# Attention scores from two fp32r parts of q and k, two heads in the two row halves of the array

## The reference, cut to what matters

```python
q = q * cos + _rotate_half(q) * sin
k = k * cos + _rotate_half(k) * sin
scores = jnp.einsum('bhqd,bhkd->bhqk', q, k) / math.sqrt(hd)
scores = jnp.where(causal[None, None], -jnp.inf, scores)
attn = jax.nn.softmax(scores, axis=-1)
attn_out = jnp.einsum('bhqk,bhkd->bhqd', attn, v)
```

## Time and profile before

| what | value |
|---|---|
| median of 3 runs | 2708.45 us (2705.41 to 2710.56) |
| span of the profiled execution, first to last instruction | 2663.3 us |
| that execution's own time | not listed apart from its span; the median stands 45.1 us above the span |
| busy: PE, DVE, ACT, GpSimd | 90%, 78%, 55%, 14% |
| projection, about | 0 to 363 us |
| routing and first max jobs, about | 363 to 437 us |
| attention loop | 437 to 2146 us |
| expert and dense networks | 2146 to 2663 us |

### The profile page before, as it was taken

One profiled execution on the slowest core, in us unless ns is written; L12 is line 12 of the kernel. 1 busy time (PEld: TensorE's weight loads), 2 busy tenths in 40 slices (PEclk: granted clock), 3 DMA queues, 4 the chain that ended last, 5 costly groups with the idle time before them and its releaser, 6 DMA issues. The chain is left out here.

```text
span 2663.3 us, 49751 instructions
## 1 busy us (share of the span) xinstructions
PE 2394.4 (90%) x14968; PEld 1211.4 (45%) x14968; DVE 2072.5 (78%) x3856; ACT 1463.1 (55%) x1762; POOL 377.9 (14%) x319
## 2 busy tenths in 40 slices
PE   0999947999999999998899999999999868886998
PEld 0889942333333333232333333333322247776888
DVE  7888889999999988562799999988864257776776
ACT  2444513566666666777566666666677733332443
POOL 2111149500000000000000000000000023333344
PEclk9999977999999999999999999999999979998999
DMA  4122247300000021000410000003100144443232
GB/s 123 64 95 91 90 114 186 104 9 9 9 9 1 9 50 43 13 10 17 92 30 9 9 9 9 1 9 70 28 9 9 22 115 126 126 126 97 64 95 71
DMA packets 158629, 144.79 MB, mean 54 GB/s; under 512 B 36448, under 2 KB 142176, under 8 KB 158304
## 3 DMA queue, kind: packets, MB, share of 16 engines
q1 hardware_dynamic: 155360, 133.94, 18.9%
q0 software_dynamic: 3072, 8.39, 0.9%
HBM read 95.61 MB, written 46.66 MB: 53 GB/s over the span
## 5 line engine op out<-in xcount | busy, mean ns | idle before, releaser
L883 DVE TENSOR_REDUCE attn_MX<-psB 128x1 f32<-128x512 f32 (+3 forms) x2352 | 1357.2, 638 | 352.5 <-PE psB L756 223.2
L869 ACT ACTIVATE attn_PB<-psB 128x1024 f32<-128x1024 f32 (+3 forms) x1152 | 1035.8, 950 | 563.9 <-PE psB L788 509.7
L756 PE MATMUL psB<-attn_KS,attn_QS 96*128 96x512 bf16 (+3 forms) x2352 | 764.5, 370 | 51.5 <-DVE attn_MX L883 44.9
L788 PE MATMUL psB<-attn_QS,attn_KS 104*128 104x512 bf16 (+3 forms) x2304 | 652.6, 363 | 24.5 <-ACT attn_QS L846 16.0
L803 PE MATMUL psB<-attn_PB,attn_V 128*32 128x512 f32 (+3 forms) x4608 | 579.8, 570 | 0.0
L756 PEld LDWEIGHTS psB<-attn_KS,attn_QS 96*128 96x128 bf16 x2352 | 200.6, 97 | 639.8 <-DVE attn_MX L883 522.2
L788 PEld LDWEIGHTS psB<-attn_QS,attn_KS 104*128 104x128 bf16 x2304 | 210.2, 98 | 336.1 <-ACT attn_PB L869 128.9
L1043 POOL TENSOR_TENSOR W1L<-W,W1H 128x512 fp32r<-128x512 f32 x36 | 53.8, 1524 | 1664.3 <-ACT W1H L1120 1664.3
L803 PEld LDWEIGHTS psB<-attn_PB,attn_V 128*32 128x32 f32 x4608 | 96.3, 108 | 175.9 <-issue 166.8
L759 PE MATMUL psB<-attn_mask_qk,attn_idb 128*128 128x128 bf16 x544 | 119.2, 227 | 0.0
L42 PE MATMUL ps_experts<-W2H,HH_experts 128*128 128x256 f32 x256 | 83.9, 328 | 35.1 <-DVE Y_experts L1233 20.3
(11 more groups left out here) (213 smaller groups left out, 3216.5 us busy)
## 6 DMA issues: line engine op xcount, KB each, us to landing
W<-in_w SPq DMA_DIRECT2D x18, 1024.0 KB, 5.5
attn_KS<-qk_parts SPq DMA_DIRECT2D x240, 64.0 KB, 3.7
attn_QS<-qk_parts SPq DMA_DIRECT2D x210, 64.0 KB, 2.8
...
```

The source lines that it names most:

```text
L756: mm = nc.tensor.matmul(ps[:, bank, 0:width], QS[0:MROW, i % 4, h, j * P:(j + 1) * P], KS[w][0:MROW, h, kc * CH:kc * CH + width], start=Tr ...
L788: mm = nc.tensor.matmul(ps[:, bank, r * P:CH], KS[w][0:KROWS, h, kb * P:(kb + 1) * P], QS[0:KROWS, i % 4, h, r * P:CH], start=True, stop=( ...
L869: nc.scalar.activation(PB[:, u % RING, 2 * pair:2 * pair + 2, r * P:CH], ps[:, 2 * (s % 2):2 * (s % 2) + 2, r * P:CH], ACT.Exp, scale=HD * ...
L883: nc.vector.tensor_reduce(MX[:, m % 4, HG * j + h, kc:kc + 1], ps[:, MB + off % 3, 0:w], AX.X, ALU.max).then_inc(reduced, 1)
```

## The change

q and k are cut into two fp32r parts instead of three bf16 ones: one cast on ACT and one subtraction on DVE for each of a chunk's four pieces, where there were two of each. Three products (high times high, high times low, low times high) and four rows for the maxima are 52 rows a head. Heads 0 and 2 of a group stand in rows 0 to 51, heads 1 and 3 in rows 64 to 115; a pair of scores and a pair of successive max jobs so lie in different row halves of the array. Matmuls of a pair of scores are issued next to each other, the two masks behind them. The rows of ones come by eight DMAs from a small tile that GpSimd fills; the query's maxima rows are zeroed by two more DMAs per load of `QS`. The numbers of max jobs, units and waits per bank, `PACE`, the mask matmuls and `weigh` stay as they are.

```diff
-        PT = sb("PT", [P, 4, 3, CH], BF16)
-        RS = sb("RS", [P, 2, CH])
+        PT = sb("PT", [P, 4, 2, CH], F32R)
...
-                    for u in range(5):
+                    for u in range(4):
                         if u == 2:
                             dve.wait_ge(xt_ready, 4 * c + 8)
                             cut(NX, 2, NXH, NXL, 2, 2 * (c + 1), xt_ready, nx_hi, nx_lo)
-                        if u < 4:
-                            dve.wait_ge(part1, 4 * c + u + 1)
-                            if u < 2:
-                                dve.wait_ge(part3, 4 * (c + 1))
-                            else:
-                                dve.wait_ge(part3, 4 * (c + 1) + u - 1)
-                            nc.vector.tensor_tensor(RS[:, u % 2, :], ps[:, QTB + u % 2, :], PT[:, u, 0, :], ALU.subtract).then_inc(rest1, 1)
-                        if u > 0:
-                            dve.wait_ge(part2, 4 * c + u)
-                            nc.vector.tensor_tensor(PT[:, u - 1, 2, :], RS[:, (u - 1) % 2, :], PT[:, u - 1, 1, :],
-                                                    ALU.subtract).then_inc(part3, 1)
-                        if u > 0:
-                            dve.wait_ge(y_ps, TPC * c + u)
-                            if u == 1:
-                                dve.wait_ge(y_out, 16 * (c + 1))
-                            nc.vector.tensor_tensor(YS[:, u - 1, :], ps[:, VB + (u - 1) % 2, 0:D], SB2[:, :], ALU.add).then_inc(y_taken, 1)
+                        dve.wait_ge(high_made, 4 * c + u + 1)
+                        nc.vector.tensor_tensor(PT[:, u, 1, :], ps[:, QTB + u % 2, :], PT[:, u, 0, :].bitcast(F32),
+                                                ALU.subtract).then_inc(low_made, 1)
+                        dve.wait_ge(y_ps, TPC * c + u + 1)
+                        if u == 0:
+                            dve.wait_ge(y_out, 16 * (c + 1))
+                        nc.vector.tensor_tensor(YS[:, u, :], ps[:, VB + u % 2, 0:D], SB2[:, :], ALU.add).then_inc(y_taken, 1)
...
-                    for u in range(5):
-                        if u < 4:
-                            act.wait_ge(qt_ps, 4 * (c + 1) + u + 1)
-                            act.wait_ge(p_out[u], 16 * (c + 1))
-                            nc.scalar.activation(PT[:, u, 0, :], ps[:, QTB + u % 2, :], ACT.Copy).then_inc(part1, 1)
-                        if u > 0:
-                            act.wait_ge(rest1, 4 * c + u + 2)
-                            nc.scalar.activation(PT[:, u - 1, 1, :], RS[:, (u - 1) % 2, :], ACT.Copy).then_inc(part2, 1)
+                    for u in range(4):
+                        act.wait_ge(qt_ps, 4 * (c + 1) + u + 1)
+                        act.wait_ge(p_out[u], 16 * (c + 1))
+                        nc.scalar.activation(PT[:, u, 0, :], ps[:, QTB + u % 2, :], ACT.Copy).then_inc(high_made, 1)
...
-PAIRS = ((0, 0), (0, 1), (1, 0), (1, 1), (0, 2), (2, 0))
-MROW = HD * len(PAIRS)
-KROWS = MROW + 2 * HG
+TILE = P // 2
+MROW, MROWS = 32, 4
+TERMS = ((0, 0, 0), (HD, 0, 1), (MROW + MROWS, 1, 0))
+KROWS = HD * len(TERMS) + MROWS
...
-        KS = [sb(f"KS{w}", [P, HG, N], BF16) for w in range(2)]
+        KS = [sb(f"KS{w}", [P, 2, N], F32R) for w in range(2)]
         V = [sb(f"V{w}", [P, NT, HG * 2 * HD]) for w in range(2)]
-        QS = sb("QS", [P, 4, HG, CH], BF16)
+        QS = sb("QS", [P, 4, 2, CH], F32R)
+        ONES = sb("ONES", [MROWS, 2, CH])
...
                 def load_q(group, i):
                     c = steps[i % LS][1]
-                    for r, (a, _) in enumerate(PAIRS):
-                        sp.dma_start(QS[HD * r:HD * (r + 1), i % 4, :, :],
-                                     qk[a, 0, bass.ds(group, 1), :, :, c * CH:(c + 1) * CH].rearrange("g d h n -> (g d) h n")).then_inc(q_in[i % 4], 16)
+                    for t in range(2):
+                        for r, a, _ in TERMS:
+                            sp.dma_start(QS[TILE * t + r:TILE * t + r + HD, i % 4, :, :].bitcast(F32),
+                                         qk[a, 0, bass.ds(group, 1), t, :, :, c * CH:(c + 1) * CH].rearrange("g d b n -> (g d) b n")).then_inc(q_in[i % 4], 16)
+                        sp.dma_start(QS[TILE * t + MROW:TILE * t + MROW + MROWS, i % 4, :, :].bitcast(F32).rearrange("p b (x n) -> p (b x) n", n=D),
+                                     zeros_row).then_inc(q_in[i % 4], 16)
                 def load_k(w, group, c):
-                    for r, (_, b) in enumerate(PAIRS):
-                        sp.dma_start(KS[w][HD * r:HD * (r + 1), :, c * CH:(c + 1) * CH],
-                                     qk[b, 1, bass.ds(group, 1), :, :, c * CH:(c + 1) * CH].rearrange("g d h n -> (g d) h n")).then_inc(kv_in[w][c], 16)
+                    for t in range(2):
+                        for r, _, a in TERMS:
+                            sp.dma_start(KS[w][TILE * t + r:TILE * t + r + HD, :, c * CH:(c + 1) * CH].bitcast(F32),
+                                         qk[a, 1, bass.ds(group, 1), t, :, :, c * CH:(c + 1) * CH].rearrange("g d b n -> (g d) b n")).then_inc(kv_in[w][c], 16)
...
+                sp.wait_ge(ones_made, 4)
+                for w in range(2):
+                    for t in range(2):
+                        for b in range(2):
+                            sp.dma_start(KS[w][TILE * t + MROW:TILE * t + MROW + MROWS, b, :].bitcast(F32).rearrange("p (x n) -> p x n", n=CH),
+                                         ONES[:, b:b + 1, :].broadcast_to([MROWS, NC, CH])).then_inc(ones_in, 16)
+                sp.wait_ge(zero_row, 1)
...
+                for b in range(2):
+                    nc.gpsimd.memset(ONES[:, b, :], float(b)).then_inc(ones_made, 1)
+                pool.wait_ge(ones_made, 2)
+                for b in range(2):
+                    nc.gpsimd.memset(ONES[0:2, b, :], float(1 - b)).then_inc(ones_made, 1)
...
-                made = 3
-                for w in range(2):
-                    for c in range(NC):
-                        part = KS[w][MROW:KROWS, :, c * CH:(c + 1) * CH]
-                        nc.gpsimd.memset(part, 0.0).then_inc(consts, 1)
-                        for first in range(2):
-                            made += 1
-                            pool.wait_ge(consts, made)
-                            nc.gpsimd.affine_select(out=part, in_=part, compare_op=ALU.not_equal, fill=1.0, base=-HG * first,
-                                                    pattern=[[-1, HG], [0, CH]], channel_multiplier=1).then_inc(consts, 1)
-                        made += 1
-                        pool.wait_ge(consts, made)
-                        pool.sem_inc(kones, 1)
...
                     if used is not None:
                         pe.wait_ge(reduced, used)
                     bank = MB + off % 3
-                    mm = nc.tensor.matmul(ps[:, bank, 0:width], QS[0:MROW, i % 4, h, j * P:(j + 1) * P],
-                                          KS[w][0:MROW, h, kc * CH:kc * CH + width], start=True, stop=(kc < c))
+                    rows, b = slice(TILE * (h % 2), TILE * (h % 2) + KROWS), h // 2
+                    mm = nc.tensor.matmul(ps[:, bank, 0:width], QS[rows, i % 4, b, j * P:(j + 1) * P],
+                                          KS[w][rows, b, kc * CH:kc * CH + width], start=True, stop=(kc < c))
                     if kc == c:
                         mm = nc.tensor.matmul(ps[:, bank, width - P:width], idb[:, :], mask_qk[:, :], start=False, stop=True)
...
                     pe.wait_ge(mparts, need)
                     if used is not None:
                         pe.wait_ge(expd, used)
-                    for j in range(TPC):
-                        mm = nc.tensor.matmul(ps[MROW:KROWS, 2 * (s % 2), j * P:(j + 1) * P],
-                                              MH[:, i % 4, j, :, :].rearrange("p s h -> p (s h)"), idb[:, :], start=True, stop=True)
+                    for t in range(2):
+                        for j in range(TPC):
+                            mm = nc.tensor.matmul(ps[TILE * t + MROW:TILE * t + MROW + MROWS, 2 * (s % 2), j * P:(j + 1) * P],
+                                                  MH[:, i % 4, j, t, :, :].rearrange("p b s -> p (b s)"), idb[:, :], start=True, stop=True)
...
                         pe.wait_ge(expd, g * S_PER + s - 1)
                     if k == 0 and pair == 0:
                         pe.wait_ge(rows_set, g * LS + i + 1)
-                    if k == 0 and pair == 1:
                         pe.wait_ge(expd, g * S_PER + (s_rows(i - 1) if i > 0 else 0) + 1)
-                    if pair == 0 and kb // TPC not in [b // TPC for b, _ in units[i][:k]]:
-                        pe.wait_ge(kones, NC * w + kb // TPC + 1)
-                    for b in range(2):
-                        h = 2 * pair + b
-                        bank = 2 * (s % 2) + b
-                        mm = nc.tensor.matmul(ps[:, bank, r * P:CH], KS[w][0:KROWS, h, kb * P:(kb + 1) * P],
```

(19 more changed lines are left out.)

50 lines of the change are left out of this document (26 added, 24 removed).

## The result

The changed kernel takes **3092.89 us** (median of 4 runs, 3080.17 to 3119.29), the kernel before 2708.46 beside it (2705.41 to 2710.56): ratio 1.143, 95% interval 1.137 to 1.148. The prediction was 2636 us, its range ended at 2745 us, and it gave the other sign. The whole loss lies in attention.

The account below looks back on a forecast made before the run. PE bounds both halves of the attention loop; afterwards DVE bounds the rising half, PE the falling. Saving 76 us in two iterations, plus 4 before the loop, gives 2591 us; a 45 us offset makes 2636 us, range 2550 to 2745.

Parts of the forecast that it names:

- Overlap, 0.114 us per matmul: Attention, max jobs and scores: two row halves run at once, so 0.114 us per 512-column matmul; ends 0.114 and 0.227.
- Rivals 3 and 4: PE: 3, halves overlap in part, 0.165 us per matmul, 2772 us, chance 0.11; 4, no overlap, some 3030 us, 0.05.
- 0.30 us per masked group: Attention, PE: each masked max job or masked score pair pays 0.30 us for tiling switches and load; ends 0 and 0.53.
- 0.095 per change: PE at masks: switching between half and full array tiling costs 0.095 us each way, the price around weigh.
- the exposed load of 0.11: PE after a tiling switch: the fp32r weight load can't be fetched ahead and adds 0.11 us, also behind each weigh.
- rival 2: PE at masks: switches dearer than around weigh, 0.53 us per masked group; 2778 us, slower; chance 0.17.
- rival 1: PE at masks: switching to halves is free, masks cost only their columns; 2570 us; chance 0.20.
- the rising half passes to DVE at 477: Attention loop, steps 0 to 8: PE's sum falls from 509 to 437 us, so DVE at 477 us bounds them.
- DVE's runs in rising steps without its 0.35 gaps: Attention, steps 0 to 8: DVE's 0.35 us idle before nine reduces goes; its busy share rises from 90 to 95%.
- The granted clock: Attention loop: if the 0.56 granted clock seen before the loop came into it, every PE term would double; no chance given.
- Prologue, +4: Before the loop (363 to 437 us): 32 masked jobs add 10 us of PE work, over half hidden; +4 us, ends 0 and 15.
- Projection, 0: Projection: DVE loses 32 subtractions and ACT 32 casts, but PE runs through; no change, at most 8 us gained.

Follow-up runs that it names:

- the kernel with masks in halves: Changed kernel with each mask added by two 64-row half-array matmuls in the head's own half instead of one whole-array matmul: 2757.07 us, ratio 1.019.
- The kernel before with changes put in: Kernel before with each mask added by two 64-row matmuls in rows 0 to 63, putting changes of the array's division around masks: 2985.37 us, ratio 1.102.
- its control: Kernel before with each mask added twice by whole-array matmuls, so no change of the array's division: 2703.58 us, ratio 1.013.

## Why the prediction was wrong

The medians differ by 384 us, the profiled executions by 3117.6 - 2663.3 = 454 us: the one after lies 27 us above its median, the one before lacks the 40 us of waits named at the start. The prediction took the 45.1 us between that span and the median for a constant offset; in the other runs an execution's own time is under 2 us above its span. The clean part is the loop without its first interval, 2067.0 - 1666.8 = 400 us, and behind the loop it is -1.

- **Overlap, 0.114 us per matmul: right.** Pairs start 4 ns apart, the next follows 0.23 us later. Its worth, freed of the rest, is 62 us (the 76 predicted were net of the masks' price). Rivals 3 and 4 are out, by the traces and by the kernel with both heads in one half. The 0.148 that the prediction worked out from the Trainium skill (TensorE: Matmul & The Clock Gate, Measured speedup vs the span model), quoted with rival 3, does not agree with 0.23 for a pair.
- **0.30 us per masked group: right** (0.26 + 0.16 against 0.06 + 0.06). So is 0.095 per change, and the exposed load of 0.11. The prediction's remark that without drains the time would be that of rival 2 is a slip: that case is rival 1.
- **The step that failed first: "the rising half passes to DVE at 477".** It set the sum of PE over a whole half (437) against that of DVE, and so let 200 groups at 0.30 = 60 us vanish under DVE. But masked groups stand together, 24 in one step of the changed kernel, and only three banks of max jobs lie between the engines. The kernel before with changes put in (32 groups a step) shows against its control that little hides: of each 0.19 us, 0.16 is on the path in the long steps, as much as in the falling ones. That the number of banks sets this is argued; no run changed it. The wait that the prediction looked for as a sign of rival 2, DVE's gaps getting wider, is what happened at the masks.
- **"DVE's runs in rising steps without its 0.35 gaps": wrong.** Nine reduces still take 6.0 us. The trace of before showed the gap and the change left its cause, the weighing. The +0.11 behind a weighing was right; the load of the max job ahead of it, which waits for DVE and then stands open (0.43 in place of 0.31), was not priced, and DVE waits for both. It took the bf16 loads to shrink the gap. This is why the long steps of the kernel with masks in halves only equal those of before (95.3 us), where 3.6 us a step less was predicted.
- **The granted clock, named at the end without price or chance, is the largest term.** Steps that the loop does twice give its price: the sixth interval between two writes takes 98.8 us with 29.1 at the lower level in one iteration and 93.2 with 13.7 in the other, the seventh 116.4 with 49.4 and 110.2 with 30.7. That is 0.36 and 0.33 us of time per us at the lower clock; seven further such pairs give 0.35 to 0.44, and the first, which has the waits, 0.72. As an estimate, (845 - 17) x 0.35 = 290 of the 400 us, which leaves some 110 us at full clock, where the prediction had -76. This rest lies evenly: 2.5 to 6.7 us in 29 of the 30 steps, so 3.7 us a step, or 0.15 us for each of 24 masked groups, near the 0.16 of the comparison with the control. So even at full clock the sign was wrong. Rival 2 had +66 us in the loop, but by a dearer group (0.53 us); the group cost 0.30, so that it names the right sign is luck. "Every PE term would double" was too strong a form: doubled throughout, a us at the lower clock would cost 0.5 us.
- **Prologue, +4: wrong, +31**, of which 18.75 is the wait shown at the start. Of the rest: the price of the copies of ones on SP was wrong. They hold its queue for 16 us from 368.6 on, PE waits 20.3 us for a DMA ahead of the first max job, and that starts at 399.4 in place of 388.6, where the prediction said that routing covers it. With bf16 parts it starts at 388.8 and the first sums are written at 438.6, against 451.0 before.
- **Projection, 0: right, to about 1 us.** The last write of the parts starts at 361.2 us in place of 362.3.

Rival 1 (free switches, 2570 us) is what the kernel with masks in halves and bf16 parts comes near (2608 us), after both were removed. No rival had two small holes that bring the clock down together.

What stays open is what it is in PE's work that makes the chip grant the lower level. The drains and the long loads bring it, each alone a little, together much; a quarter fewer rows in the max jobs don't, more streaming in one half doesn't undo it. No run separated the share of the clock from that of the holes themselves; the 290 us are a slope from pairs of steps.
